# Attention values and their sums moved between partitions by DMA instead of PE transposes, with a finer placement table

## The reference

```python
q = (x @ w_q.T).reshape(B, S, 16, 16); k = x @ w_k.T; v = x @ w_v.T      # one key and value head, 16 query heads
attn = softmax(einsum('bshd,btd->bhst', q, k) * scale)
a = einsum('bhst,btd->bshd', attn, v).reshape(B, S, 256) @ w_out.T
x1 = layernorm(x + a)
x2 = layernorm(x1 + gelu(x1 @ ternary(W1).T + b1) @ ternary(W2).T + b2)
# second layer: a state space part (cumulative sum over the positions), then a recurrence over all 512 positions
#   h = ff1 * (1 - t) + t * ff2, with ff1, ff2, t from tanh and sigmoid of [x_t, h] @ w.T
x3 = layernorm(x2 + (x2 + h @ out_w.T + out_b))
out = layernorm(x3 + dequantised(x3 in fp6 blocks of 32) @ dequantised(weight).T + bias)
```

## Time and profile before

| | us |
|---|---|
| runs of before | 2025.29, 2027.75, 2032.19 (median 2027.75) |
| the profiled execution | 2027.62, of which span 2025.9 |
| PE busy | 1832.2 (90%) |
| DVE busy | 1456.5 (72%) |
| ACT busy | 1203.1 (59%) |
| POOL busy | 1006.3 (50%) |
| granted PE clock, mean | 0.971 |

### The profile page before, as it was taken

One profiled execution on the slowest core, in us unless ns is written; L12 is line 12 of the kernel. 1 busy time (PEld: TensorE's weight loads), 2 busy tenths in 40 slices (PEclk: granted clock), 3 DMA queues, 4 the chain that ended last, 5 costly groups with the idle time before them and its releaser, 6 DMA issues.

```text
span 2025.9 us, 74372 instructions
## 1 busy us (share of the span) xinstructions
PE 1832.2 (90%) x29791; PEld 1258.9 (62%) x29791; DVE 1456.5 (72%) x3040; ACT 1203.1 (59%) x2845; POOL 1006.3 (50%) x3190
## 2 busy tenths in 40 slices
PE   6869999999999999999999999999999999999875
PEld 3525566666666666666666666666666666666653
DVE  5867767777777777777777777777777777777455
ACT  4636666656666666656666666656665666666521
POOL 1002235555555555555555555555555555555542
PEclk8979999999999999999999999999999999999975
DMA  7311111111111111111111111111111111111000
GB/s 205 90 27 33 38 37 39 41 44 42 42 38 47 39 45 38 44 40 44 42 39 45 41 43 36 47 39 44 40 42 41 44 42 38 47 39 28 18 26 20
DMA packets 138224, 89.78 MB, mean 44 GB/s; under 512 B 19748, under 2 KB 137560, under 8 KB 137880
## 3 DMA queue, kind: packets, MB, share of 16 engines
q1 hardware_dynamic: 137880, 85.03, 15.6%
HBM read 29.67 MB, written 16.78 MB: 23 GB/s over the span
## 4 chain that ended last, share of the span: by engine, by line
PE 61%; DVE 20%; issue 6%; POOL 6%; ACT 4%; SPq 1%; DMA 1%; DVEq 0%; POOLq 0%; ACTq 0%
PE gen_bank L734 11%; DVE nmax L1252 9%; PE gen_bank L832 9%; PE value_bank L696 8%; PE score_bank L654 8%; PE max_banks L682 7%; PE gate_bank L728 4%; PE gen_bank L550 3%; DVE stats L1175 3%; PE gate_bank L712 3%; POOL mixed L1531 2%; ACT probs L965 2%; PE gen_bank L789 2%; PE gen_bank L748 1%; DVE x2r L1238 1%
## 5 line engine op out<-in xcount | busy, mean ns | idle before, releaser
L1252 DVE TENSOR_REDUCE nmax<-max_banks 128x2 f32<-128x1024 f32 x512 | 623.9, 1219 | 228.1 <-PE max_banks L684 225.9
L965 ACT ACTIVATE probs<-score_bank 128x512 f32<-128x512 f32 x1024 | 593.8, 596 | 323.3 <-PE score_bank L654 321.6
L654 PE MATMUL score_bank<-qaug,kaug 98*128 98x512 bf16 x1024 | 379.6, 385 | 3.3 <-ACT probs L965 2.0
L696 PE MATMUL value_bank<-probs,vaug 128*32 128x128 f32 x8192 | 330.8, 279 | 0.0
L696 PEld LDWEIGHTS value_bank<-probs,vaug 128*32 128x32 f32 x8192 | 192.9, 109 | 162.8 <-issue 114.5
L1528 POOL TENSOR_TENSOR diff<-gates 128x16 f32<-128x16 f32 x472 | 109.5, 232 | 295.8 <-ACT gates L970 289.5
L734 PE MATMUL gen_bank<-w2T,hT 128*128 128x256 f32 x1024 | 248.9, 386 | 0.0
L682 PE MATMUL max_banks<-kaug,qaug 64*128 64x512 bf16 x512 | 200.9, 392 | 35.6 <-DVE nmax L1252 28.4
L734 PEld LDWEIGHTS gen_bank<-w2T,hT 128*128 128x128 f32 x1024 | 189.6, 190 | 35.6 <-issue 13.8
L728 PE MATMUL gate_bank<-hseq,ghT 128*32 128x16 f32 x11328 | 172.2, 183 | 37.3 <-POOL hseq L1533 37.3
L728 PEld LDWEIGHTS gate_bank<-hseq,ghT 128*32 128x32 f32 x11328 | 160.2, 112 | 66.7 <-POOL hseq L1533 65.2
(11 more groups left out here) (232 smaller groups left out, 3001.4 us busy)
## 6 DMA issues: line engine op xcount, KB each, us to landing
qstage<-qpiece SPq DMA_DIRECT2D x384, 64.0 KB
lowstage<-qpiece SPq DMA_DIRECT2D x192, 64.0 KB
xt<-in_L_attn_x SPq DMA_DIRECT2D x64, 128.0 KB
xk<-in_L_attn_x SPq DMA_DIRECT2D x16, 512.0 KB, 6.4
residual<-x2s SPq DMA_DIRECT2D x64, 128.0 KB
x2f<-residual SPq DMA_DIRECT2D x64, 128.0 KB
out<-x SPq DMA_DIRECT2D x64, 128.0 KB
raw<-in_L_ffn_W SPq DMA_DIRECT2D x2, 1024.0 KB, 9.7
```

Of the source, the lines that this page charges most:

```text
L654: pe.matmul(score_bank[t % 2][:, :], kaug[0:AUG, 4 * r + u, tt * P:(tt + 1) * P], qaug[:, r, u, :, :].rearrange("p h s -> p (h s)"), start ...
L696: last = pe.matmul(value_bank[32 * g:32 * g + 32, :].rearrange("p (k t) -> p k t", k=HG)[:, :, uv * BLOCK_POS:(uv + 1) * BLOCK_POS], vaug[ ...
L965: act.activation(probs[:, t % 4, :], score_bank[t % 2][:, :], ACT.Exp).then_inc(exp_done, 1)
L1252: dve.tensor_reduce(nmax[:, (r + lead) % 2, at:at + 3:2], max_banks[:, :, :], AX_X, ALU.max, negate=True).then_inc(max_taken, 1)
```

## The change

- `TICKS` stay 16, but the tables now count **slots**, four to a tick (`SLOTS = 64`). On PE, ACT and POOL slots 4t and 4t+1 come ahead of the odd-tick work (values, recurrence step, maxima), slots 4t+2 and 4t+3 behind it; on DVE all four come behind the maxima.
- The second FFN layer goes from four pieces (F2A to F2D) to eight (F2_0 to F2_7), spread from tick 14 to tick 6 of the next tile time (slots 56 to 90). X2R and LN2 move with it, from ticks 2 and 1 to tick 6; POOL's `both_factors` is split in `outer_factor` (LN2) and `inner_factor` (LNI). The gelu is split in GELUA and GELUB.
- The PE transposes OT and ATT, the ACT copy of ATT, and the tiles `att` and `rsum` of 16 columns go. In their place ACT copies `oT` once more into `spread` (SPREAD, 128x512), SP issues eight DMAs of 16 partitions x 256 elements that bring values and sums to matching partitions (`move_values`, behind `move_queries`), and DVE takes the reciprocal of 128x256 sums and multiplies 128x256 values straight into `attT` (ATT, slot 32, which is tick 8). PROJ moves from tick 6 to tick 10.
- In the setup, `w_q` comes with two DMAs instead of one, and `w_out` with one instead of four that had runs of 16 elements.

```diff
-PE_AT = dict(XT=4, INPUT=1, Q=0, OUT=5, OT=2, ATT=3, PROJ=6, TURNX=9, B=10, X1T=10, NM=12, FFN1A=14, FFN1B=14, TURND=18, LAST=19, F2A=15, F2B=15, F2C=18, F2D=18)
-DVE_AT = dict(Q=0, X2R=2, X3R=7, X2=5, OT=3, X3=13, QUANT=15, XN=9, ORDER=10, LN1=7, X1=9, BS=11, SCAN=15, X1P=12, NM=12, X4R=21, X4=27)
+PE_AT = dict(XT=4, INPUT=1, Q=0, OUT=27, PROJ=40, TURNX=42, B=44, X1T=47, NM=52, FFN1A=52, FFN1B=54, TURND=73, LAST=83, F2_0=56, F2_1=56, F2_2=56, F2_3=62, F2_4=75, F2_5=77, F2_6=87, F2_7=90)
+DVE_AT = dict(Q=0, X2R=27, X3R=27, X2=45, X3=54, QUANT=57, XN=35, ORDER=32, LN1=39, X1=42, BS=45, SCAN=61, X1P=45, NM=50, X4R=83, X4=90, ATT=32)
...
+            def move_values(m):
+
+                sp.wait_ge(values_spread, m + 1)
+                settle(sp)
+                for g in range(GROUP):
+                    low, high = slice(32 * g, 32 * g + DK), slice(32 * g + DK, 32 * g + 2 * DK)
+                    sp.dma_start(spread[high, 0, :, :], oT[low, KT:HG, :]).then_inc(values_moved, 16)
+                    sp.dma_start(spread[low, 1, :, :], oT[high, 0:KT, :]).then_inc(values_moved, 16)
...
                 if live(n + LEAD["Q"]) and n >= 0:
                     move_queries(n + LEAD["Q"])
+                if live(n + LEAD["FFN"]):
+                    move_values(n + LEAD["FFN"])
...
+                        m = mine("SPREAD", "FFN")
+                        if m is not None:
+                            act.wait_ge(values_out, m + 1)
+                            settle(act)
+                            act.activation(spread[:, :, :, :], oT[:, :, :].rearrange("p (c k) t -> p c k t", k=KT),
+                                           ACT.Copy).then_inc(values_spread, 1)
...
+                        m = mine("ATT", "FFN")
+                        if m is not None:
+                            dve.wait_ge(values_moved, 32 * GROUP * (m + 1))
+                            settle(dve)
+                            if m > 0:
+                                dve.wait_ge(filled[0], use(0, "PROJ", m - 1) + 1)
+                            dve.reciprocal(rsum[:, :, :], spread[:, 1, :, :]).then_inc(att_step, 1)
+                            dve.wait_ge(att_step, m + 1)
+                            dve.tensor_tensor(attT[:, :, :], spread[:, 0, :, :], rsum[:, :, :], ALU.mult).then_inc(att_made, 1)
...
-            for m in range(KT):
-                for k in range(KT):
-                    sp.dma_start(raw_o[:, m, :].rearrange("p (h k d) -> p h k d", k=KT, d=DK)[:, :, k, :],
-                                 w_out[m * P:(m + 1) * P, k * P:(k + 1) * P].rearrange("p (h d) -> p h d", d=DK)).then_inc(loaded["o"], 16)
+            sp.dma_start(raw_o[:, :, :], w_out.rearrange("(m p) e -> p m e", p=P)).then_inc(loaded["o"], 16)
```

More of the change, by code:

```diff
@@ L18 @@
 TICKS = 16
+SLOTS = 4 * TICKS
 STEPS = 8
@@ L795, in general @@
-                m = mine("PROJ", "FFN")
-                if m is not None:
-                    pe.wait_ge(emptied[0], use(0, "PROJ", m))
-                    for k in range(KT):
-                        last = pe.matmul(g0[:, 0:D], attT[:, k, :], woT[:, k, :], start=(k == 0), stop=(k == KT - 1))
-                    last.then_inc(filled[0], 1)
-                m = mine("TURNX", "SSM")
-                if m is not None:
-                    pe.wait_ge(emptied[1], use(1, "TURNX", m))
-                    pe.wait_ge(ln_done[LNI], m + 1)
-                    turn_tile(g1, xn).then_inc(filled[1], 1)
@@ new lines, in general @@
+                    m = mine("PROJ", "FFN")
+                    if m is not None:
+                        wait(pe, emptied[0], use(0, "PROJ", m))
+                        pe.wait_ge(att_made, m + 1)
+                        for k in range(KT):
+                            last = pe.matmul(g0[:, 0:D], attT[:, k, :], woT[:, k, :], start=(k == 0), stop=(k == KT - 1))
+                        last.then_inc(filled[0], 1)
+                    m = mine("TURNX", "SSM")
+                    if m is not None:
+                        pe.wait_ge(emptied[1], use(1, "TURNX", m))
+                        pe.wait_ge(ln_done[LNI], m + 1)
+                        turn_tile(g1, xn).then_inc(filled[1], 1)
@@ new lines, in general @@
+                    m = mine("B", "SSM")
+                    if m is not None:
+                        pe.wait_ge(emptied[1], use(1, "B", m))
+                        pe.wait_ge(emptied[1], use(1, "TURNX", m) + 1)
+                        for k in range(KT):
+                            last = pe.matmul(g1[:, 0:P], bwgT[:, k, :], xnT[:, k, :], start=(k == 0), stop=(k == KT - 1))
+                        last.then_inc(filled[1], 1)
+                    m = mine("X1T", "FFN")
+                    if m is not None:
+                        pe.wait_ge(emptied[0], use(0, "X1T", m))
+                        pe.wait_ge(ln_done[LN1], m + 1)
+                        turn_tile(g0, x1).then_inc(filled[0], 1)
@@ L1007, in tile_time @@
-                    m = mine("FFN1", "FFN")
-                    if m is not None:
-                        for half, name in enumerate(("FFN1A", "FFN1B")):
-                            act.wait_ge(filled[half], use(half, name, m) + 1)
-                            for f in range(4):
-                                ft = 4 * half + f
-                                last = act.activation(hT[:, ft, :], gen_bank[half][:, f * P:(f + 1) * P], ACT.Gelu, bias=cols[:, C_B1 + ft:C_B1 + ft + 1])
-                            last.then_inc(emptied[half], 1)
+                    work(range(4 * t + 2, 4 * t + 4))
```

531 lines of the change are left out of this document (265 added, 266 removed).

## The result

The changed kernel takes 2396.1 us (median of 4 runs, 2394.8 to 2396.8), the kernel before, beside it, 2027.9 us. The ratio is 1.181, with a 95% interval of 1.179 to 1.183: 368 us slower. The profiled execution has a span of 2394.4 us.

What follows compares the result with a forecast made beforehand. PE's own list was taken as the present bound; after the change a chain of 15.7 + 7.7 + 7.4 = 30.8 us a tile time against 28.57, +143 us over 64 tile times, less 4 in setup, gave 2170 us; range 2045 to 2285.

Steps and rivals of the forecast that it cites:

- DVE ready at 14.0: On DVE, its list reaches the reciprocal's place about 14.0 us after the start of the query product.
- SP's start at 3.35: On SP, the query transfers begin to issue 3.35 us after the start of the query product.
- Values landed at 15.7: Value transfers, queued behind nine query transfers on SP, land 15.7 us after the query product starts; bounds 13.7 to 17.1.
- Reciprocal of 1755 ns: On DVE, the reciprocal of 256 elements a partition takes 1755 ns, drawn from two traced reciprocals.
- Reciprocal to `x1r`, 3.75: On DVE, reciprocal, product and gaps take 2.25 us, then ordering copies and `xn` 1.5; PROJ runs beside these.
- `x1r` to the first FFN layer, 3.95: From `x1r` on DVE to the first FFN layer: 2.2 to `x1`, then 0.45, 0.8 and 0.5 us.
- First FFN layer to the next query product, 7.4: On PE, a dense stretch of FFN halves, values to maxima, four second-layer blocks and three score products takes 7.4 us.
- clock held: Main case: values land late, PE's granted clock stays up; 2170 us, own range 2110 to 2225, chance 0.42.
- The case in which it falls: Rival: PE's clock falls in the idle time before PROJ, +64 to +128 us more, 2230 to 2300; chance 0.20.
- values early: Rival: values land at 13.7 to 14.3, DVE is the bound; tile time 29.1 to 29.5, 2060 to 2085 us; chance 0.20.
- PE bound and faster: Rival: PE's list stays the bound and only loses its transposes and the wait ahead of them; 1955 us; chance 0.14.
- The setup's 4 us: In the setup, the shorter `w_out` loading on SP saves 4 us once.

Runs made afterwards that it cites:

- E1: Changed kernel without the eight value transfers, the reciprocal waiting for ACT's copy instead (result incomplete): 2180.0 us.
- E4: Changed kernel with eight unneeded products of 128x256 on PE ahead of its wait for `attT` before the projection: 2365.3 us.
- E11: E1 with three unneeded products of 128x256 on PE ahead of the output projection: 2111.6 us.
- E6: Changed kernel without the eight value transfers and with a multiplication by a constant in place of the reciprocal (result incomplete): 2039.1 us.
- E7: E1 with eight unneeded products of 128x256 on PE ahead of the output projection: 2214.9 us.
- E8: Kernel before with `w_out` read in one load, its columns left in the load's order (result wrong): 2024.7 us, ratio 0.9988.
- E9: Changed kernel with SP's order four queries, eight values, five queries, and DVE's query ordering in slot 36 instead of 32 (result complete): 2241.7 us.
- E12: Kernel before with `w_out` in one load and `att` written in that column order, whole result computed: 2023.8 us, ratio 0.9988.

## Where the prediction was right, and where it was wrong

The sign and the chain were right: slower, by a wait of DVE for the values, then the reciprocal, then a dense stretch to the next query product. The size was not: 2170 forecast, 2045 to 2285 as the range, 2396 measured. In a tile time 30.8 was forecast and 34.3 came. Step by step, from the query product (measured are the means of the table):

- **DVE ready at 14.0**: 13.84 in E1, where nothing holds it. Right. SP's start at 3.35: 3.46 in the timeline (1020.58 to 1024.04). Right.
- **Values landed at 15.7**: the reciprocal starts at 17.1, so this term is short by 1.4 us. It sits just at the upper bound that I gave. The landing itself was faster than assumed (1.8 us in the median against 2.3). It was the issuing: from the first to the end of the last I counted 5.9 for nine and 7 x 0.59 + 0.54 for eight, 10.6 us, and SP takes 12.2 in the mean, because in every tile time one or two issues take some 0.4 to 1.8 us longer than the 0.6 of the others. From the first query issue to the first value issue it is 6.6 us where I had 5.9, and from there to the last value issue 5.1 where I had 4.1. The earlier trace rows is a single tile time, in which nine took 5.9, and I took it for all of them: in the kernel before they take 6.2 in the mean, from 5.7 to 7.1.
- **Reciprocal of 1755 ns**: 1752. Right, and drawn from two shapes of the same operation. The estimate of 3.4 us from the Trainium skill, VectorE: DVE Perf Modes, First, the fixed hardware budget, is twice what is measured, and the measurement decides.
- **Reciprocal to `x1r`, 3.75**: 4.44 (2.36 + 2.08), short by 0.7. I had the projection done before DVE came to `x1r`. At 2.04 us instead of 1.03 it isn't, and DVE waits 0.73 for it. That is the clock: E4 takes 0.70 off P to X, and R to X is 3.65 there and in E11.
- **`x1r` to the first FFN layer, 3.95**: 4.74, short by 0.8. It is 4.30 wherever the clock holds without transfers (E6, E7, E11), and 4.28 in the tile times of E4 in which it holds, so about 0.45 goes with the clock. The other 0.35 lies in three of the terms: in E11 2.39 from `x1r` to `x1` where I had 2.20, 0.56 from there to X1T where I had 0.45, and 0.86 from X1T to `x1rest` where I had 0.8.
- **First FFN layer to the next query product, 7.4**: 8.04, short by 0.65, and between 7.97 and 8.12 in every row of the table that has it, whatever the clock does before it. All of it is in the first FFN layer, which holds PE for 3.3 us and not the 2.68 of the earlier trace rows: behind the first 16 of its products PE waits for the later pieces of x1 (0.25 us idle at 1013.94, and slow starts around it). What follows takes the 4.7 us that I counted.

The misses are 1.4 + 0.7 + 0.8 + 0.65 = 3.5 us, and 30.8 + 3.5 = 34.3. Times 64 they are 224 us, and 2170 + 224 = 2394. By cause they are 1.4 us from the issuing on SP, some 1.2 from the clock, and 1.0 from the two stretches put together from single rows.

**The steps that failed** are then two: the landing of the values at 15.7 us (measured 17.1), and "clock held" as the main case. The first is a term that was sized from one tile time. The second failed by judgement. The case in which it falls had a chance of 0.20 and 2230 to 2300 us. Its mechanism is what happened, in each tile time: 0.50 after the wait for `attT`. The prediction itself had PE idle for some 3 us ahead of the projection in each tile time, and rows that showed the clock at 0.50 after a gap of 3 us; to give "clock held" twice the chance was against its own rows. The Trainium skill, TensorE: Matmul & The Clock Gate, HAM oscillation, has a wait for a transfer in each round of a loop throwing PE back to the low clock in each; this trace agrees, with 0.50 from 1004 to 1010 and again from 1038 to 1044 us. By price the rival was near: 64 to 128 us more forecast, 68 us measured in E1 against E11, and 31 in E4, whose products held the clock in only half of the tile times. But the clock alone doesn't fill the gap: even 2300 is 96 us short. The second error is that the range took the unfavourable cases one at a time. Late landing (at its bound of 17.1) with the fallen clock gives 34.2 a tile time by the prediction's own numbers (17.1 + 7.7 + 7.4 + 2.0), nearly what came. These two aren't independent, since a later landing makes the gap on PE longer.

The other rivals: *values early* (2060 to 2085) falls, since DVE waits 3.2 us. But the premise that this would leave 29.1 to 29.5 a tile time falls too, for in E1 the reciprocal has no wait at all and a tile time takes 30.9, and 29.7 with the clock held (E11). *PE bound and faster* (1955) falls with E6, where neither transfers nor the reciprocal are in the way: 2039, 28.57 us a tile time. What bounds E6 with 2.35 us of idle PE in a tile time was not tried. *The setup's 4 us*: in the two profiled executions the first query product of the tile times starts 4.1 us earlier (115.5 against 119.6), but among the executions with one load of `w_out`, in the same setup as the changed kernel, that start lies anywhere from 114.7 to 118.6, so one pair can't show the size. E8 measures 3.1 us less for the whole, with an interval of 0.4 to 4.7 us. That is right in sign and agrees in size.

## What to carry to other kernels

A small transfer has a price in its queue (0.6 us an issue here) and not only a landing time: seventeen issues took 12 us of each tile time, and the place of the eight among them decided over 154 us (E9). Reordering only moves the wait, though, once the queue is too long for everything that stands behind it: in E9 it went over to the query transfers. Before work leaves an engine that is the bound for a chain that goes once round all engines, add up that chain with all bad ends at once: wait, longer instruction and lower clock come together. And where PE waits a microsecond or two in each round of a loop, look at the granted clock behind the wait, in every round and not in one; a few products of no use in the wait, just as many as fit, were worth 68 us in one kernel (E11) and cost 35 when there were too many (E7).

## What the runs showed of the hardware

- In E1, with PE busy 91% of the time and idle for at most 1.5 us at a stretch, the granted clock fell to 0.50 around the output projection in each of 39 tile times, for three to seven microseconds; the two stretches shown have 0.59 and 0.55. Three products of 128x256 in the wait kept it at 1.00 in all 40 (E11). In E4 eight products ahead of a wait that was still 1.3 us long kept it in 18 of 35.
- POOL's power takes 41.1 us for 128x256 numbers and 0.57 to 0.7 us for 128x1. Its products of 128x256 take 0.6 to 0.8 us in the same traces.
- Among SP's seventeen issues in a row some take 1.2 to 2.1 us instead of 0.6; the largest issue of a value transfer was 1.86 us, the median 0.59. Why was not tried.
- DVE's product with a pattern of four dimensions takes 425 ns, as long as with three (E12).
